# Summing a head's four partial results on TensorE instead of VectorE, one step earlier

## The reference

```python
x = x + 0.5 * ffn(layernorm(x), Wg, A, B)
x = x + attn(layernorm(x), Wq, Wk, Wv, Wr, u_bias, v_bias)
x = x + 0.5 * ffn(layernorm(x), Wg, A, B)

# attn: 16 heads of 16 channels for each of the 2 sequences
AC = einsum('bhid,bhjd->bhij', q + u_bias, k)
BD = rel_shift(einsum('bhid,hjd->bhij', q + v_bias, rp))
attn = softmax((AC + BD) * scale)
out = einsum('bhij,bhjd->bhid', attn, v)
```

## Time and profile before

| | |
|---|---|
| three runs | 3274.0 us median (3268.14 to 3276.89) |
| the profiled execution's own time | 3274.0 us |
| its span, first to last instruction | 3272.1 us |
| TensorE busy in the span | 89% |
| VectorE, ScalarE, GpSimd busy | 82%, 76%, 71% |
| mean granted TensorE clock | 0.944 of 2.4 GHz |

### The profile page before, as it was taken

The page is one execution under the profiler, slowest core; times in us unless marked ns, Lnnn a source line. Parts: engine busy times, 40 slices in busy tenths (PEclk is TensorE's granted clock), DMA queues, the critical chain, the costliest instruction groups (busy, mean ns, idle before and its releaser), DMA issues. The chain is left out here.

```text
span 3272.1 us, 109617 instructions
## 1 busy us (share of the span) xinstructions
PE 2904.6 (89%) x40256; PEld 1994.5 (61%) x40256; DVE 2687.9 (82%) x5170; ACT 2500.8 (76%) x3850; POOL 2310.1 (71%) x4135
## 2 busy tenths in 40 slices
PE   4556479999999999998999999999999999999955
PEld 1444146666666666665666666666666666666635
DVE  2555158989898989897989998989989898989976
ACT  2333468988888888887888888888888888888832
POOL 3333487878787878786878888777878787878810
PEclk8777679999999999999999999999999999999987
DMA  6233688888888888887888888888888888888841
GB/s 197 95 110 96 147 210 220 223 220 219 210 223 216 225 210 218 219 221 189 222 225 220 232 218 221 218 214 216 224 222 220 219 218 218 222 221 223 214 127 52
DMA packets 290217, 657.25 MB, mean 201 GB/s; under 512 B 189472, under 2 KB 256928, under 8 KB 272288
## 3 DMA queue, kind: packets, MB, share of 16 engines
q0 software_dynamic: 190960, 526.89, 61.5%
q1 hardware_dynamic: 98736, 123.38, 13.4%
HBM read 77.19 MB, written 46.14 MB: 38 GB/s over the span
## 5 line engine op out<-in xcount | busy, mean ns | idle before, releaser
L665 POOL DMA_DIRECT2D score<-score x3999 | 2178.3, 548 | 578.0 <-ACT score L900 508.0
L898 ACT COPY score<-pos_bank 128x512 f32<-128x512 f32 x2048 | 1104.0, 596 | 331.6 <-PE pos_bank L773 329.2
L908 ACT ACTIVATE score<-score,low 128x1024 f32<-128x1024 f32 x1024 | 1196.7, 1170 | 36.6 <-DVE low L961 32.3
L970 DVE COPY prob_t<-pt_bank 128x512 f32<-128x512 f32 x1792 | 1161.5, 684 | 5.0 <-PE pt_bank L840 5.0
L840 PE MATMUL pt_bank<-ident_sb,score 128*128 128x128 f32 x8192 | 1095.8, 276 | 11.1 <-issue 6.9
L840 PEld LDWEIGHTS pt_bank<-ident_sb,score 128*128 128x128 f32 x8192 | 947.9, 142 | 253.2 <-DVE prob_t L970 75.5
L961 DVE CUSTOM_DVE_ANT_0 score<-ac_bank,score 128x1024 f32<-128x1024 f32 x512 | 627.1, 1225 | 265.6 <-DMA score<-score 153.4
L773 PE MATMUL pos_bank<-pos,qv 96*32 96x512 bf16 (+15 forms) x12160 | 665.5, 318 | 53.2 <-DMA qv<-qv_parts 42.6
L961 DVE CUSTOM_DVE_ANT_0 score<-ac_bank,score,low 128x1024 f32<-128x1024 f32 x512 | 657.3, 1284 | 49.1 <-PE ac_bank L826 35.5
L826 PE MATMUL ac_bank<-ks,qu 96*128 96x512 bf16 x2048 | 626.8, 388 | 78.3 <-DVE low L961 69.6
L854 PE MATMUL acc_bank<-prob_t,vs 128*32 128x128 f32 x16384 | 667.7, 280 | 10.9 <-issue 10.8
(11 more groups left out here) (96 smaller groups left out, 1024.3 us busy)
## 6 DMA issues: line engine op xcount, KB each, us to landing
score<-score POOLq DMA_DIRECT2D x3937, 129.5 KB, 5.3
pos<-pos_parts SPq DMA_DIRECT2D x96, 128.0 KB, 9.9
qv<-qv_parts SPq DMA_DIRECT2D x192, 64.0 KB, 7.2
ks<-k_parts SPq DMA_DIRECT2D x192, 64.0 KB, 7.5
qu<-qu_parts SPq DMA_DIRECT2D x192, 64.0 KB, 7.2
v_heads<-v_sb SPq DMA_DIRECT2D x8, 1024.0 KB, 7.3
vs<-v_heads SPq DMA_DIRECT2D x32, 256.0 KB, 6.9
pos_parts<-part SPq DMA_DIRECT2D x16, 384.0 KB, 2.7
```

The costliest lines, as they stand in the source:

```text
L665: pool.dma_start(shifted(odd, s, groups, 0), shifted(odd, s, groups, QUAD - 1 - s))\
L898: act.copy(score[:, at + f, c * BANK:(c + 1) * BANK], ring(m)[:, :]).then_inc(pos_out, 1)
L908: act.activation(cols, cols, ACT.Exp, bias=low[:, slot(k), NH - 1:NH], scale=-1.0)\
L970: dve.tensor_copy(prob_t[:, c, :], PT[c % 2][:, :]).then_inc(copied, 1)
```

## The change

The fold becomes a matmul of `acc_sb` with `fold_sb`, which transposes and sums the four quarters at once and leaves 32 columns for each tile in the bank. VectorE's reduction and its buffer `sums` go; the reciprocal and the product read the bank directly. The bank is handed back by `fin_used`, the count of the product, in place of `summed`. TensorE runs `fold` ahead of `content` instead of behind it. VectorE runs `finish` behind the first `add` of the third tile and ahead of that half's two copies.

```diff
@@ positions
-                            pe.wait_ge(summed, group(step, i) + 1)
+                            pe.wait_ge(fin_used, group(step, i) + 1)
@@ fold
-                        pe.wait_ge(summed, group(step, j))
+                        pe.wait_ge(fin_used, group(step, j))
                     for f in range(FT):
-                        last = pe.matmul(POS[FOLD_AT % 3][:, f * P:(f + 1) * P],
-                                         lhsT=acc_sb[:, f * P:(f + 1) * P], rhs=ident_sb[:, :], is_transpose=True,
-                                         start=True, stop=True)
+                        last = pe.matmul(POS[FOLD_AT % 3][:, f * VW:(f + 1) * VW],
+                                         lhsT=acc_sb[:, f * P:(f + 1) * P], rhs=fold_sb[:, :], start=True, stop=True)
@@ TensorE's body
+                        if h and k % FT == 1 and group_there(step, fold_no(k)):
+                            fold(step, k)
                         if there(step, k + AC_AHEAD + h):
                             content(step, k + AC_AHEAD + h, 1 - h)
-                        if h and k % FT == 1 and group_there(step, fold_no(k)):
-                            fold(step, k)
@@ finish
-                    quarters = POS[FOLD_AT % 3][:, :].rearrange("p (f c w) -> p f w c", f=FT, w=VW)[:, :, 0:DH + 1, :]
-                    dve.tensor_reduce(sums[:, :, :], quarters, AX.X, ALU.add).then_inc(summed, 1)
-                    dve.wait_ge(summed, group(step, j) + 1)
-                    dve.reciprocal(rden[:, :], sums[:, :, DH]).then_inc(inverted, 1)
+                    fin = POS[FOLD_AT % 3][:, 0:FT * VW].rearrange("p (f w) -> p f w", w=VW)
+                    dve.reciprocal(rden[:, :], fin[:, :, DH]).then_inc(inverted, 1)
...
-                    dve.tensor_tensor(head_out[:, h % 2, j % FT * FT:j % FT * FT + FT, :], sums[:, :, 0:DH],
+                    dve.tensor_tensor(head_out[:, h % 2, j % FT * FT:j % FT * FT + FT, :], fin[:, :, 0:DH],
@@ VectorE's body
                     if there(step, n):
                         add(step, n, 0)
+                    if k % FT == 2 and group_there(step, fold_no(k)):
+                        finish(step, k)
                     for h in range(NH):
-                        if h and k % FT == 2 and group_there(step, fold_no(k)):
-                            finish(step, k)
                         if h and there(step, n):
                             add(step, n, 1)
```

More of the change, by code:

```diff
@@ L556, in build_program @@
             rden = s2("rden", [P, FT])
-            sums = s2("sums", [P, FT, DH + 1])
             head_out = s2("head_out", [P, 2, NI, DH])
@@ L576, in build_program @@
             acc_out, fin_full, fin_used, inverted = sem("acc_out"), sem("fin_full"), sem("fin_used"), sem("inverted")
-            summed = sem("summed")
             block = c2.enter_context(nc.Block())
```

## The result

The changed kernel takes 3305.76 us (median of 4 runs, 3298.59 to 3311.43) against 3275.43 us before (4 runs); the ratio is 1.0103 with a 95% interval of 1.0087 to 1.012. It is slower: by 30 us between the two medians, by about 34 us by the ratio. The forecast was 3271 us, no measurable change. The profiled execution took 3308.99 us with a span of 3307.2.

A forecast was written before the change was run, and what follows sets the result against it. VectorE leads from a group's first add, and TensorE stands still 0.35 us per group. DMA-waiting groups -9.6, ordinary +8.3, last groups -1.8, together -3.1 us: 3274.0 becomes 3271 us, range 3256 to 3290.

The forecast's parts named there:

- F: TensorE time of the fold's four matmuls ahead of content: each as long as its 0.108 us load, 0.45 us together.
- the DMA waits: VectorE's waits for shifted rows: 38 groups keep theirs, 33 gain 0.29 us each, 52 ordinary groups lose 0.16 each.
- The upper bound of F: The fold's four matmuls if load and matmul ran one after the other: 0.54 us, total 3276 us, chance 0.08.
- rival 2: Slower: transfers' rate sets when rows land, so gain behind DMA waits vanishes; if waits shrink too, 3292 us; chance 0.18.
- A: Start of VectorE's first add after W; predicted at W + 0.85 + F, since content runs behind the fold.
- W: When TensorE finishes positions of the second tile's second half; fourth tile's turn forecast 6.23 us later, 6.07 before.
- The finish: VectorE's finish without reduction, ahead of the copies: 0.37 us, fourth tile's turn 4.93 us behind the add instead of 5.22.
- Rival 3: Slower: VectorE's small reads from PSUM cost 0.12 us more in 85 groups, +10 us, 3281 us; chance 0.08.
- The wait for the bank: Positions get their bank back at about A + 1.6, needed after A + 3; costs nothing, at most 0.37 us.
- Both signs: Wrong if the fold's four matmuls take other than 0.4 to 0.5 us, or DMA waits change by over 10 us.
- Rival 4: VectorE's time bounds the whole kernel: its busy time falls by 55 us and the span too, to 3219; chance 0.04.
- Rival 1: Weight loads hide beside matmuls: F is 0.24 us or less, an ordinary group gains 0.05 us, 3260 us; chance 0.15.

The follow-up runs named there:

- the two kernels at 6.13: The changed kernel with both orders put back, 3264.83 us (ratio 0.9977), and with only the fold put back behind content, 3272.81 us (ratio 1.0001).

## Why the prediction was wrong

**The step that failed** is the term F, "each of the four takes the longer of the two, 0.108 us, ... 4 x 0.108 plus a few ns is F = 0.45 us". The price of a load was right (0.107 to 0.11 in the eight of the change), the count was half: F measured 0.91. The rows on record had shown it: in the earlier trace rows the transposes L840 count 8192, which is 512 tiles x 16, while the loads of L854, also 16 a tile in the source, count 16384. The run with half the folds shows how far this one count reaches: F = 0.47, ratio 1.0005. With F = 0.91 the prediction's own sum has 0.62 us for each of its 52 ordinary groups, +32.2 in place of +8.3, and gives 3295 us. The other 11 us up to the measured 3306 belong to a second step, the count of groups that pay (under the DMA waits below).

**The upper bound of F** (0.54) was worked out from load and matmul in series and not from the count, so no F in the prediction came near 0.91; the range's upper end, 3290, came from rival 2 and was too low too. Load and matmul in series fall as well: with the right count they would be 8 x (0.108 + 0.027) = 1.08 us.

**The mechanism of the move** held: A fell back by F, and the queue behind the fold did the damage. The prediction's own distance, 6.23 us, missed the measured 6.63 by the error in F. All seven distances from W to the turn that were given before an experiment, with the profile of the change then known, met the measured ones within 0.07 us.

**The finish** held: 0.36 against 0.37 us, 4.88 against 4.93 from the add to the turn. Rival 3 falls: the reciprocal takes 177 ns from PSUM and the product 225, 179 and 225 from SBUF before (the earlier trace rows has the product, this row the reciprocal). The Trainium skill's 62 extra cycles for a read of PSUM (VectorE: DVE Perf Modes, section The TRN2 errata — SBUF-src ops pay a fixed extra latency per instruction) do not show here.

```profile
L979 DVE RECIPROCAL rden<-sums 128x4 f32<-128x4 f32 x128 | 22.9, 179 | 4.4
```

**The wait for the bank** by `fin_used` cost nothing: in the waits of TensorE no row names VectorE's product.

**The DMA waits** were treated too coarsely. The prediction let 38 groups keep their waits whatever the others lost, and only 52 groups pay. Measured, only 16 waits are left when the groups are this much longer, and nearly every group pays. With the average loss of 0.65 us, 124 x 0.65 = 80, less 42.5 of shorter waits, less 1.8 at the end, are 36 us, against 35 between the two profiled executions. (With the 0.56 of the one group shown the sum stops at 25.) The sum doesn't follow every wait: over the first 123 groups W to turn, its waits included, grew by 44 us in all, and the rest of the groups shrank by 11, which no run explains.

This is the second half of rival 2, "if the waits also shrink to take no cover, every group loses", for which the prediction had 0.18 together with its first half. The experiments go the same way: the waits inside the attention sum to 118.3 us in the kernel with the cut finish (W to turn 5.73), 106.1 with the bfloat16 fold (5.83), 94.0 before (6.07), 76.0 with half the folds (6.19), 56.4 with only the finish put back (6.51), 51.5 with the change (6.63) and 49.5 with the orders alone (6.69). Only the two kernels at 6.13, with 101 us each, are out of this order. A shorter group mostly brings more waiting, a longer one is partly repaid. That the transfers' own rate sets when the rows land, as rival 2 has it, fits this and is not shown by itself. Both signs that the prediction named for being wrong came: the fold outside 0.4 to 0.5 us, and the waits changed by over 10 us.

**Rival 4** (VectorE's total is the bound) is refuted by the result itself: VectorE became 61 us less busy and the program slower. Rival 1 expected the error in F on the other side, F below 0.45.

## What to carry to other kernels

Take the number of instructions of a matmul from a trace of the same form, not from the source: here each ordinary float32 matmul is two loads and two matmuls, a transpose one of each, so "one matmul that also sums" costs twice the transpose that it replaces (0.91 against 0.44 us), with 32 moving columns and about the same with 128. When two engines hand work to each other, ask what queues behind a step: the same eight matmuls cost a group 0.06 us behind the instruction that VectorE waits for and 0.56 us ahead of it. An engine that is idle now and then is filled by cutting a step so that each piece fits one wait: here that gained 0.6%, while taking the reduction out at its old place, at the price of the doubled fold, gained 0.2%. And where a program waits for transfers in some rounds, a loss in the others shows only in part, as does a gain.

## What the runs showed of the hardware that was not expected

A float32 load of 128 x 128 (0.84 ns a column) and the move of 128 columns (0.86 ns a column, both worked out from the earlier trace rows) take about the same 0.11 us each, twice for every ordinary float32 matmul of the fold (eight in 0.99 us with 128 moving columns, 0.91 with 32); in bfloat16 four loads with their matmuls fit into 0.11 us altogether. The Trainium skill's page FP8 and Floating Point Precision, section TensorE Precision Notes, says that true float32 takes four passes through the array. The trace doesn't show passes. It agrees if each instruction counts as two of them: two instructions at 0.86 ns a column, near the 0.83 ns of two cycles of 2.4 GHz.
